# An attention and feed-forward layer on one core: the down projection as three f32r products of high and low parts

## What is computed

```python
x = x + xattn(layernorm(x), ctx, ctx, bias, key_padding_mask, w_in, b_in, w_out, b_out)
x = x + ffn(layernorm(x), w_gate, w_up, w_down)

def fp4_linear(x, w):            # blocks of 16 along the last dim
    return einsum('bsk,nk->bsn', fp4_quant_dequant(x), fp4_quant_dequant(w))

def ffn(x, w_gate, w_up, w_down):
    h = silu(fp4_linear(x, w_gate)) * fp4_linear(x, w_up)
    return fp4_linear(h, w_down)
```

## Time and profile before

| | |
|---|---|
| median of 3 runs | 930.79 us (929.17 to 930.88) |
| the profiled execution | 930.9 us, span 928.9 us |
| busy, share of the span: TensorE / its weight loads | 95% / 76% |
| VectorE / ScalarE / GpSimd | 76% / 67% / 58% |
| granted TensorE clock, mean | 0.993 of full |
| instructions at L1584 (down product) | 384, 91.7 us busy, mean 380 ns |
| chain that ended last: TensorE / ScalarE / VectorE | 79% / 6% / 4% |

### The profile page before, as it was taken

One profiled execution on the slowest core, in us unless ns is written; L12 is line 12 of the kernel. 1 busy time (PEld: TensorE's weight loads), 2 busy tenths in 40 slices (PEclk: granted clock), 3 DMA queues, 4 the chain that ended last, 5 costly groups with the idle time before them and its releaser, 6 DMA issues.

```text
span 928.9 us, 20211 instructions
## 1 busy us (share of the span) xinstructions
PE 883.6 (95%) x6772; PEld 706.7 (76%) x6772; DVE 710.6 (76%) x1866; ACT 617.8 (67%) x1119; POOL 534.8 (58%) x501
## 2 busy tenths in 40 slices
PE   5699999999999999999999999999889999999997
PEld 5577777787777777777787777777568888888886
DVE  3868678677677776776776679899579999989984
ACT  2377677777677776777776777787755555555542
POOL 5677867776696687677678557875203222222222
PEclk9799999999999999999999999999999999999999
DMA  6577334442442534344243343610000000000000
GB/s 193 150 221 205 113 72 126 103 117 71 114 116 60 146 86 102 98 100 132 74 115 103 72 134 73 174 35 1 1 1 12 18 18 19 21 17 17 18 18 29
DMA packets 50796, 76.50 MB, mean 82 GB/s; under 512 B 5264, under 2 KB 22032, under 8 KB 50704
## 3 DMA queue, kind: packets, MB, share of 16 engines
q1 hardware_dynamic: 50448, 75.06, 29.9%
q10 hardware_dynamic: 256, 0.26, 0.1%
HBM read 45.16 MB, written 29.36 MB: 80 GB/s over the span
## 4 chain that ended last, share of the span: by engine, by line
PE 79%; ACT 6%; issue 6%; DVE 4%; POOL 2%; DMA 2%; SPq 1%; ACTq 0%; DVEq 0%
PE psum L1233 26%; PE psum L1377 11%; PE psum L1331 11%; PE psum L1584 9%; PE psum L1569 4%; PE psum L1568 4%; PE psum L1567 4%; PE psum L1295 3%; PE psum L1255 2%; ACT att L776 2%; DVE att L1089 2%; PE psum L1261 2%; ACT att L783 1%; PE psum L1272 1%; ACT att L727 1%
## 5 line engine op out<-in xcount | busy, mean ns | idle before, releaser
L1089 DVE CUSTOM_DVE_ANT_0 att<-psum,att 128x512 f32<-128x512 f32 x512 | 341.7, 686 | 143.3 <-PE psum L1331 141.4
L618 POOL TENSOR_TENSOR att<-att,neg_max 128x512 f32<-128x512 f32 x308 | 322.4, 1057 | 172.8 <-DVE neg_max L1089 170.4
L1233 PE MATMUL psum<-ident,att 128*128 128x128 f32 x2576 | 380.8, 276 | 25.2 <-ACT att L776 8.2
L1233 PEld LDWEIGHTS psum<-ident,att 128*128 128x128 f32 x2576 | 311.6, 142 | 93.0 <-ACT att L776 30.2
L776 ACT ACTIVATE att<-psum 128x512 f32<-128x512 f32 x512 | 298.3, 599 | 117.7 <-PE psum L1233 113.4
L1331 PE MATMUL psum<-stack 128*128 128x512 f32 x512 | 251.2, 492 | 10.5 <-DMA stack<-q_hl 7.2
L783 ACT ACTIVATE att<-att,neg_max 128x512 f32<-128x512 f32 x204 | 147.2, 722 | 13.4 <-DVE neg_max L1089 13.4
L701 POOL TENSOR_TENSOR att<-att 128x704 f32<-128x704 f32 x32 | 61.8, 1931 | 162.8 <-DVE att L1211 162.8
L1331 PEld LDWEIGHTS psum<-stack 128*128 128x128 f32 x512 | 97.8, 191 | 43.9 <-issue 32.3
L1377 PE MATMUL psum<-att 128*32 128x256 f32 x2048 | 123.8, 382 | 0.0
L1584 PE MATMUL psum<-att 128*128 128x256 f32 x384 | 91.7, 380 | 2.7 <-ACT att L903 2.7
(11 more groups left out here) (104 smaller groups left out, 1066.3 us busy)
## 6 DMA issues: line engine op xcount, KB each, us to landing
stack<-qk_planes SPq DMA_DIRECT2D x124, 192.0 KB, 3.9
qk_planes<-k_hl SPq DMA_DIRECT2D x48, 256.0 KB
qk_planes<-q_hl SPq DMA_DIRECT2D x48, 256.0 KB
att<-in_fside_1xSxS_dram SPq DMA_DIRECT2D x32, 256.0 KB, 2.8
att<-in_ctx_dram SPq DMA_DIRECT2D x8, 512.0 KB, 7.4
out_dram<-att SPq DMA_DIRECT2D x32, 128.0 KB, 1.7
x<-in_x_dram SPq DMA_DIRECT2D x1, 2560.0 KB, 13.5
x<-in_x_dram SPq DMA_DIRECT2D x3, 512.0 KB, 6.5
```

The costliest lines, as they stand in the source:

```text
L618: pool.tensor_tensor(prob[:, slot, :], prob[:, slot, :], neg_max[:, slot:slot + 1].to_broadcast([P, S]), ALU.subtract).then_inc(less_pool, 1)
L1089: dve.tensor_tensor_reduce(out=prob[:, slot, :], in0=ps_score[:, SCORE_BANK[2 * S_ + r], :], in1=bias_m[:, tt, :], scale=-1.0, scalar=BIG, ...
L1233: return pe.transpose(out_, in_, ident[:, :])
```

## The change

The down product goes from six f32 products to 18 f32r products: for each of six chunks of 128 rows, h high x w high, h high x w low, and, after all of these, h low x w high. For that:

- ScalarE copies `ps_h` twice, first to an f32r tile (`hqT_hl[..., 0, :]`, the high part, in a `stack` slot that is free by then), then in f32 to `f_hT`. `fhT_taken` comes after the second; the second waits for GpSimd to have read the `f_hT` of the tile before.
- GpSimd subtracts the high part from `f_hT` (128x768, all in SBUF, output f32r), ahead of its L701 of that step. It waits for `fhT_taken`.
- TensorE runs the 12 products with h high after `fhT_taken`, then L1594, then waits for `fhlow_ready` and runs the six products with h low.
- The down weights are kept as high part (in `kv_hl`) and low part (two places); the low parts are made by VectorE in the last batch, for pieces 0 to 2, which it left out before.
- `RING` goes from 13 to 12 and `att` shrinks, to make room.

```diff
-    RING = 13
+    RING = 12
...
-            pool.memset(w_dnT[:, IC - 1, :], 0.0).then_inc(vv_zero, 1)
+            pool.memset(kv_hl[:, 4 * EC * S:].bitcast(F32), 0.0).then_inc(vv_zero, 1)
...
             def step(n, par):
+                m = n - 3
+                if live(m):
+                    pool.wait_ge(fhT_taken, m + 1)
+                    wait(pool, fdn_ready, m - 1)
+                    pool.tensor_tensor(hqT_hl[:, 1 - par, 1, :], f_hT, hqT_hl[:, 1 - par, 0, :].bitcast(F32),
+                                       ALU.subtract).then_inc(fhlow_ready, 1)
                 m = n - 2
...
                     wait(act, fdn_ready, m - 1)
-                    act.activation(f_hqT[:, 1 - par, :, :].rearrange("p c t -> p (c t)"), ps_h[:, 0:IC * P], ACT.Copy).then_inc(fhT_taken, 1)
+                    if isinstance(m, int) and m == 0:
+                        act.wait_ge(score_ready, TILES * N_OCT)
+                    act.activation(hqT_hl[:, 1 - par, 0, :], ps_h[:, 0:IC * P], ACT.Copy)
+                    wait(act, fhlow_ready, m)
+                    act.activation(f_hT, ps_h[:, 0:IC * P], ACT.Copy).then_inc(fhT_taken, 1)
...
                 dve.wait_ge(gwT_taken, z + 1)
+                if g == 2:
+                    src = bank.rearrange("p (c n) -> p c n", c=2)
+                    if m < IC - 2:
...
+                        dve.wait_ge(k_plane, 48 * N_OCT)
+                        dve.tensor_tensor(w_dn_low4[:, m:m + 2, :], src, w_dn_high[:, m:m + 2, :].bitcast(F32), ALU.subtract).then_inc(gw_low, 1)
+                    else:
+                        dve.tensor_tensor(w_dn_low2[:, 0, :], src[:, 0, :], w_dn_high[:, m, :].bitcast(F32), ALU.subtract)
+                        dve.tensor_tensor(w_dn_low2[0:ILAST, 1, :], src[0:ILAST, 1, :], w_dn_high[0:ILAST, m + 1, :].bitcast(F32),
+                                          ALU.subtract).then_inc(gw_low, 1)
+                    return
...
-                def down(m, chunks):
-                    for c in chunks:
-                        last = pe.matmul(ps_y[:, 1 - par, :], f_hqT[:, 1 - par, c, :], w_dnT[:, c, :],
-                                         start=c == 0, stop=c == IC - 1)
-                    return last
-
                 if live(n - 3):
+
                     pe.wait_ge(fhT_taken, n - 2)
                     wait(pe, fout_ready, n - 3)
-                    down(n - 3, range(0, IC // 2))
+                    for c in range(IC):
+                        high = hqT_hl[:, 1 - par, 0, c * P:(c + 1) * P]
+                        pe.matmul(ps_y[:, 1 - par, :], high, w_dn_high[:, c, :], start=c == 0, stop=False)
+                        pe.matmul(ps_y[:, 1 - par, :], high, w_dn_low(c), start=False, stop=False)
...
                 if live(n - 3):
-                    down(n - 3, range(IC // 2, IC)).then_inc(fdn_ready, 1)
+                    pe.wait_ge(fhlow_ready, n - 2)
+                    for c in range(IC):
+                        last = pe.matmul(ps_y[:, 1 - par, :], hqT_hl[:, 1 - par, 1, c * P:(c + 1) * P], w_dn_high[:, c, :],
+                                         start=False, stop=c == IC - 1)
+                    last.then_inc(fdn_ready, 1)
```

More of the change, by code:

```diff
@@ L86, in xattn_ffn @@
         neg_half = sb("neg_half", [P, NT])
-        att = sb("att", [P, 28352])
+        att = sb("att", [P, 26816])
         used = [0]
@@ L121, in xattn_ffn @@
         oT = cut(EC, S)
-        at_w_dn = used[0]
-        w_dnT = cut(IC, E)
+        w_qT = cut(EC, E)
         w_outT = cut(EC, E)
@@ L126, in xattn_ffn @@
         bo_bc = cut(E)
-        w_qT = att[:, at_w_dn:at_w_dn + EC * E].rearrange("p (c e) -> p c e", c=EC)
         w_nat = probT.rearrange("p a b c d -> p (a b c d)")[:, 0:8 * E].rearrange("p (c e) -> p c e", c=8)
@@ L158, in xattn_ffn, with w_dn_low @@
         w_gu_high = stack[:, (2 * N_OCT - 3) % SLOTS, :, :, :].rearrange("p x k s -> p (x k s)")[:, 0:EC * GU].rearrange("p (c n) -> p c n", c=EC)
-        kv_hl = sb("kv_hl", [P, 4 * EC * S], F32R)
+        AT_DN = EC * GU
+        kv_hl = sb("kv_hl", [P, AT_DN + (IC + 2) * E], F32R)
         ctxT_high, ctxT_low, w_kv_high, w_kv_low = (
             kv_hl[:, i * EC * S:(i + 1) * EC * S].rearrange("p (c s) -> p c s", c=EC) for i in range(4))
-        assert 2 * E == S and EC * GU <= 4 * EC * S
+        assert 2 * E == S and 4 * EC * S <= AT_DN + (IC + 2) * E
+        w_dn_high = kv_hl[:, AT_DN:AT_DN + IC * E].rearrange("p (c e) -> p c e", c=IC)
+        w_dn_low2 = kv_hl[:, AT_DN + IC * E:].rearrange("p (c e) -> p c e", c=2)
+        w_dn_low4 = k_hl.rearrange("p a s -> p (a s)").rearrange("p (c e) -> p c e", c=IC - 2)
+        def w_dn_low(c):
+            return w_dn_low4[:, c, :] if c < IC - 2 else w_dn_low2[:, c - IC + 2, :]
         w_gu_low = kv_hl[:, 0:EC * GU].rearrange("p (c n) -> p c n", c=EC)
@@ L194, in lows_of @@
         def lows_of(z):
-            return sum(1 for i in range(z) if piece_rows(i)[0] < 2)
+            return z
         used[0] = at_bias
@@ L216, in xattn_ffn @@
         f_hq = cut(2, IC * P)
-        f_hqT = cut(2, IC, P)
+        f_hT = cut(IC * P)
         f_out = cut(2, E)
         assert used[0] <= at_bias
+        assert 4 * IC * P == 6 * S
+        hqT_hl = stack[:, (2 * N_OCT - 1) % SLOTS, :, :, :].rearrange("p x k s -> p (x k s)").rearrange(
+            "p (i j n) -> p i j n", i=2, j=2)
         psum = cx.enter_context(nc.psum_tensor("psum", [P, 8, 512], F32))
@@ L282, in xattn_ffn @@
         fhu_ready, fhd_ready, fhq_ready = sem("fhu_ready"), sem("fhd_ready"), sem("fhq_ready")
-        fhT_ready, fhT_taken = sem("fhT_ready"), sem("fhT_taken")
+        fhT_ready, fhT_taken, fhlow_ready = sem("fhT_ready"), sem("fhT_taken"), sem("fhlow_ready")
         fdn_ready, fout_ready = sem("fdn_ready"), sem("fout_ready")
@@ L763, in take_weights @@
                 elif m < IC - 2:
-                    act.activation(w_dnT[:, m:m + 2, :], src, ACT.Copy).then_inc(gwT_taken, 1)
+                    act.activation(w_dn_high[:, m:m + 2, :], src, ACT.Copy).then_inc(gwT_taken, 1)
                 else:
-                    act.activation(w_dnT[:, m, :], src[:, 0, :], ACT.Copy)
-                    act.activation(w_dnT[0:ILAST, m + 1, :], src[0:ILAST, 1, :], ACT.Copy).then_inc(gwT_taken, 1)
+                    act.activation(w_dn_high[:, m, :], src[:, 0, :], ACT.Copy)
+                    act.activation(w_dn_high[0:ILAST, m + 1, :], src[0:ILAST, 1, :], ACT.Copy).then_inc(gwT_taken, 1)
             def exp_tile(n, s, r):
@@ L1026, in weights_low @@
                 g, m = piece_rows(z)
-                if g == 2:
-                    return
                 c0, cols = g * I + m * P, min(2 * P, I - m * P)
                 dve.wait_ge(gwT_taken, z + 1)
+                if g == 2:
[8 more added lines that the diff above has]
+                    return
                 dve.tensor_tensor(w_gu_low[:, :, c0:c0 + cols], bank.rearrange("p (c n) -> p c n", c=2)[:, :, 0:cols],
```

## The result

| | before | after |
|---|---|---|
| median | 930.84 us (929.17 to 931.35, 4 runs) | 964.08 us (961.91 to 964.29, 4 runs) |
| ratio, 95% interval | | 1.0355 (1.0335 to 1.0375) |
| the profiled execution | 930.9, span 928.9 | 961.9, span 960.1 |
| granted clock, mean | 0.993 | 0.991 |

The account below looks back on a forecast made before the run. TensorE bounds the feed-forward at 7.40 us a tile; VectorE was to become the bound at 8.42. Loop 27.0, ends 4.7 and last batch 1.9 sum to 33.6 on 930.8: 964, range 946 to 976.

Parts of the forecast that it names:

- The bound: Feed-forward tiles: passes from TensorE, 7.40 us a tile, to VectorE, 8.42, with TensorE waiting 1.5 a tile.
- TensorE's part: Feed-forward down product: 18 f32r products at 0.115 replace 2.59 us, tile 7.40 to 6.9 (8.5 at the upper bound).
- ScalarE's second copy: Feed-forward, copy of 768 columns from PSUM: 0.71 us a tile, hidden in 0.93 idle ahead of the silu.
- The subtraction: GpSimd's new 128x768 instruction per feed-forward tile: 1.87 us, between 1.5 and 1.93; 1.66 by the skill's figure.
- The port: SBUF access of VectorE and GpSimd: changes hands at each instruction, loser waits for the whole one; 1.78 us a tile lost.
- rival B: VectorE keeps the port through its unbroken run, L1202 to L1215; period 7.85, 949 us; chance 0.14.
- rival C: The subtraction and VectorE's L1202 to L1215 don't block each other, or under 0.77; 6.9 a tile, 922 us; chance 0.09.
- the free stretch: VectorE's L1160, L1163 and L1167, one SBUF operand or none, 1.93 us: L701 falls there, the subtraction can't as well.
- VectorE's step: VectorE's work per feed-forward tile: 6.64 us, plus 1.78 blocked, makes 8.42, 1.0 a tile over 7.40.
- The ends and the last batch: Last feed-forward tiles +4.7 us (3.9 and 0.8); four VectorE instructions for low weights +1.9 in the last batch.
- Rival D: Subtraction and L701 both fall in VectorE's unbroken run; 9.8 us a tile, 1002 us; chance 0.07.

Follow-up runs that it names:

- e2_gpsimd_writes: Changed kernel with GpSimd's subtraction replaced by fills about as long that read no SBUF, low part of h left zero: 924.05 us, ratio 0.9932, period 6.95.
- e7_two_h: Changed kernel with two buffers for the product h, so VectorE's L1189 need not wait for the L1244 before it: 961.99 us, ratio 1.0345.
- e5_half_low: Changed kernel with GpSimd subtracting only three of six chunks (384 columns) and three low products instead of six: 936.31 us, ratio 1.0065.
- e9_free_stretch: Changed kernel with GpSimd rescaling first, subtracting right behind, VectorE's step reordered, low products and output one step later: 938.49 us, ratio 1.0098.
- e6_two_products: Changed kernel without w_down's low part, in the last batch and in the product (12 matmuls instead of 18): 962.58 us, ratio 1.0349.

## Why the prediction was right

**The bound** passed from TensorE to VectorE, as forecast; TensorE's waits are for VectorE by way of L717.

**TensorE's part.** 18 products at 0.119 instead of 0.115, a tile of 6.95 (`e2_gpsimd_writes`) instead of 6.9. Right. Of the 1.4 that it has to spare, 1.03 shows as idle ahead of the transposes, and another 0.15 is the drain of the last product (0.87, where six products that are followed at once take 0.72 in `e2_gpsimd_writes`); the remaining 0.2 isn't taken apart.

**ScalarE's second copy** is hidden, as forecast.

**The subtraction** takes 1.85 for the forecast 1.87. By the Trainium skill (GPSIMD Engine Reference, "3.1 Elementwise") it would have been the estimated 1.66; the measurement is 11% above that. The subtractions of 384 and of 768 columns take 1.01 and 1.85, which is 2.2 ns a column and a fixed part of about 0.17. The first agrees with the 2.6 cycles an element, at 1.2 GHz, that the Trainium skill gives there; the estimate left out the second.

**The port.** That it changes hands at each instruction, so that rival B's uninterrupted run doesn't exist, is shown by `e7_two_h`, and by four tiles of the changed kernel: the subtraction gets in between L1231 and L1236, which had no gap. That reads are what excludes is shown by `e2_gpsimd_writes`, and rival C, on the other side, falls with the changed kernel itself; its 922 is nearly what `e2_gpsimd_writes` reaches. By the rule of the Trainium skill (SBUF - State Buffer, "Who interferes with whom") the one that comes second is fully blocked; 2.37 for 0.88 and 2.06 for 0.41 agree. One row that the prediction read as evidence for the hand-over is of another kind. L959 at 40.18 reads one SBUF tensor and two columns of numbers, one per partition, so it isn't an instruction with two SBUF tensors, and by the prediction's own split it should have run through. In the kernel before:

```profile
L959 DVE TENSOR_SCALAR att<-x,mean_var,rstd x32: 400/408/1133, 9.6 to 460.6; 128x256 f32<-128x256 f32 x32
```

Of its 32 runs, 14 start while GpSimd's L618 is running: 13 of these take 0.73 to 1.13, one takes 0.41; the other 18 take 0.40 to 0.41. So one SBUF tensor or two isn't the whole of the rule. Of the instructions with at most one, the runs clear the kinds that stand in the free stretch: one operand in PSUM, the maxima, the reciprocal.

**Two terms of VectorE's step were mis-sized, in opposite directions.** The block is 1.49, not the 1.78 taken (1.76 with the subtraction first). Of the 0.27 less than 1.76, 0.14 is a larger head start (the subtraction starts 0.23 ahead of L1231, forecast were 0.09), and 0.13 is that L1231 ends only 0.75 behind the subtraction, 0.13 less than the 0.88 that it takes undisturbed. `e5_half_low` gives the same 0.13 (1.01 - 0.22 - 0.66). Missing was the 0.21 that VectorE waits for its own L1244. In the kernel before it was hidden in the 0.78 of idle time; once VectorE is the bound, it counts. 6.64 + 0.21 + 1.49 = 8.34, where the prediction had 6.64 + 1.78 = 8.42. Per tile 0.93 instead of 1.0, or 25.1 instead of 27.0.

**The ends and the last batch** were too low by 1.0 (5.7 for 4.7) and 0.45 (2.35 for 1.9). The runs show the second to be the low weights, all of it. Of the first, the two periods ahead of the last two grew by 0.56 for the forecast 0.1, and the last two by 4.42 for 3.8. The very last is 6.15 for 5.8, and there the clock has a part:

```profile
948.00:952.00 4.00, 3.65 (x18) 3.65 (x19) 0.00 (x0) 0.30 (x1) 3.17 (x2) 0.57 0.00 0
```

TensorE had stood idle for 1.60 until 948.36; over these four us the granted clock is 0.57, its products start 0.21 apart instead of 0.12, and the last transposes start at 952.08, 0.53 behind the end of L717, in the loop 0.05. In `e7_two_h`, with the clock at 1.00 there, the same period is 5.74. So 964.0 owes its closeness to errors that cancel: 1.9 too much in the loop, 1.5 too little outside it.

**Rival D** (both GpSimd instructions in the run) didn't occur: L717 takes 1.97 as before, as L1244 holds the port when it asks.

**What stays open.** Beside VectorE's step runs a loop of waits that is as long in the changed kernel: from the subtraction over L1231 to L1244, the rescaling, the transposes and two copies back to the subtraction, 1.85 + 2.55 + 1.38 + 0.97 + 1.60 = 8.35. `e7_two_h` was meant to tell the two apart and didn't: taking 0.21 from VectorE only turned the race at the port, so that its step came to 8.29, and the loop of waits to as much. Both need the subtraction inside the run, so the cause isn't in doubt; which of the two would bind without the other is.

## What to carry to other kernels

Work handed to an idle GpSimd isn't free if it reads SBUF while VectorE works on two SBUF tensors: most of its length is taken from VectorE (here 1.49 to 1.65 of 1.85). Look first where in VectorE's step the two will meet, then whether an engine that reads PSUM can do it (VectorE 0.87, TensorE with ScalarE 7.31 - 6.95 = 0.36), or whether it can be moved beside instructions that read one SBUF tensor or none and that a trace shows to be undisturbed there (L959 above is one that isn't). In reordering, put no instruction right behind the one whose result it reads. And when an edit makes another engine the bound, that engine's small waits, hidden until then, join the sum.

## What the runs showed of the hardware

- A fill by GpSimd, which reads no tensor, blocks no VectorE instruction with two SBUF operands (0.89 and 0.88 beside fills in `e2_gpsimd_writes`), while a subtraction of about the same length costs 1.49 to 1.65.
- A VectorE instruction with one SBUF tensor and two columns of per-partition numbers can be shut out as well (L959, 0.73 to 1.13 for 0.40).
- An instruction of VectorE that reads what the one just ahead wrote starts about 0.12 later than an independent one (0.40 for 0.28, 0.46 for 0.34, in `e9_free_stretch`), and 0.2 to 0.3 later behind one of 704 columns, also where it only overwrites what that one reads (1.08 for 0.80, 1.02 for 0.80).
- TensorE made less busy was granted less clock: `e6_two_products`, with a third of the down products gone, had a mean of 0.974, and its window reads

```profile
770.00:870.00 100.00, 83.97 (x466) 72.41 (x465) 98.34 (x169) 58.90 (x108) 47.35 (x24) 0.95 0.05 16
```

  where the changed kernel's has 87.45 at 1.00, the 2.4 GHz level; a mean of 0.95 says that a part of the window was granted the 1.2 GHz level only. Though VectorE is the bound, it wasn't free: 1.1 over the 27 periods and 1.3 behind them, about what the run had saved in the last batch.
